# Unread 512-column bfloat16 products in TensorE's order, from the routing stage to the first slots

## The chip, the cores and the metric

The program runs on one core of a Trainium2 chip. The metric is the device time of one execution in microseconds. Three runs of the kernel before gave 3014.59, 3015.5 and 3016.41 us, a median of 3015.5 us.

## The reference, cut to what matters

Four layers are added to `x` (8 x 256 tokens of 256 numbers) one after the other. The first is attention with a context of 1601 rows, the second an expert layer with two of eight experts, the third a masked attention over the context, and the fourth an expert layer in which each token goes to one expert of eight. Only the fourth is touched:

```
x = _layernorm(x)
route = sigmoid(x @ router_w)                 # 2048 x 8
max_ind = argmax(route, axis=1)
max_prob = route[max_ind]
for e in range(8):
    h = silu(x @ gate_w[e]) * (x @ up_w[e])   # 256 -> 512
    out = out + where(max_ind == e, h @ down_w[e], 0)   # 512 -> 256
out = out * max_prob
```

## The kernel before, in words

The program is a row of blocks. In a block each engine has its own list of instructions, and between two blocks all engines meet at a barrier. Two blocks matter here.

`route_to_slots` decides which token goes to which expert. The 2048 tokens lie as 16 tiles of 128. VectorE (DVE) and GpSimd (POOL) make mean and deviation, and VectorE writes the normalised tiles `xn`. TensorE (PE) works in eight turns of two tiles. `turn(g)` (L2376 to L2383) transposes four 128x128 pieces into `ps_t`, ScalarE (ACT) copies them to `xt` (L2416), and four products with `router_w`, eight columns wide, put the router's sums into `ps_l` (L2392). A float32 product is two passes on the array, so that the trace has eight records for these four. `turn(g + 1)` stands ahead of the products of turn g, and so ScalarE's copy lies beside TensorE's work.

Then ScalarE applies the sigmoid (L2418), and VectorE picks each token's best expert and writes `onehot_bf`. TensorE counts the tokens of each expert (`ps_n`, L2397 and L2399, one and 16 products in bfloat16). VectorE turns the counts into a slot and a lane for each token: at most 23 slots of 128 rows, each of one expert. TensorE collects by 16 float32 products (`ps_f`, L2407) which token stands where, and VectorE writes `read_at` and `write_at` from it. Meanwhile SyncE (SP) has issued the loads of all expert weights, 12 MB (L2270).

`moe_slots` works through the 23 slots. GpSimd gathers the 128 rows of a slot by an indirect DMA (L2458), VectorE normalises them (`xn`, L2559), TensorE transposes them (`turn_x`, `ps_x`, L2480), ScalarE copies them, and TensorE multiplies by the gate and up weights (`hidden`, `ps_g` and `ps_u`, L2492), transposes the hidden rows (`ps_h`, L2501) and multiplies by the down weights (`ps_y`, L2509). The list of TensorE opens with `turn_x(0)`, `turn_x(1)`, a wait for the weights, and `hidden(0)`.

TensorE takes its instructions strictly in the written order. It stands at a wait until the semaphore has its value, and whatever stands ahead of an instruction must be through before it.

Of the kernel before, what the change touches and what calls it, by code (L numbers as in the profile page):

```python
# [14 lines left out]
P = 128  # L15
# [2191 lines left out]
def route_to_slots(nc, x_sb, router_dram, weights_dram, weights, w_loaded, mean_var, rstd, half, ident, upper_bf, ones_bf, iota,  # L2207
# [3 lines left out]
    with ExitStack() as ctx:  # L2211
        sb, psum, sem = scope(ctx, nc)
# [36 lines left out]
        ps_l = psum("ps_l6", [P, NT * E1])  # L2249
        ps_n = psum("ps_n6", [P, (NT + 1) * E1])  # L2250
        ps_f = psum("ps_f6", [P, FACTS * ESLOTS])

        router_loaded, upto_ready, tokens_made = sem("router6_loaded"), sem("upto6s"), sem("tokens6_made")
        xn_ready, xt_ready, xt_copied, logits, scored = sem("xn6s"), sem("xt6s"), sem("xt6_copied"), sem("logits6"), sem("scored6")
# [9 lines left out]
        with nc.Block() as block:  # L2264
            @block.sync
            def _(sp):
                sp.dma_start(router[:, :, :], router_dram.rearrange("(c p) e -> p c e", p=P)).then_inc(router_loaded, 16)

                for dst, src in zip(weights, weights_dram):
                    sp.dma_start(dst[:, :, :, :], src.rearrange("e (c p) n -> p e c n", p=P)).then_inc(w_loaded, 16)  # L2270
# [100 lines left out]

            @block.tensor
            def _(pe):
                pe.wait_ge(router_loaded, 16)

                def turn(g):  # L2376
                    pe.wait_ge(xn_ready, 2 * g + 2)
                    if g >= 2:
                        pe.wait_ge(xt_copied, g - 1)
                    for t in range(2):  # L2380
                        for c in range(DC):
                            last = nc.tensor.transpose(ps_t[:, g % 2, (t * DC + c) * P:(t * DC + c + 1) * P], xn[:, 2 * g + t, c * P:c * P + P], ident[:, :])
                    last.then_inc(xt_ready, 1)  # L2383

                turn(0)
                for g in range(NT // 2):
                    if g + 1 < NT // 2:
                        turn(g + 1)
                    pe.wait_ge(xt_copied, g + 1)
                    for t in range(2):  # L2390
                        for c in range(DC):
                            last = nc.tensor.matmul(ps_l[:, (2 * g + t) * E1:(2 * g + t + 1) * E1], xt[:, g % 2, (t * DC + c) * P:(t * DC + c + 1) * P],  # L2392
                                                    router[:, c, :], start=c == 0, stop=c == DC - 1)
                    last.then_inc(logits, 1)

                pe.wait_ge(is_own_bf, 1)
                nc.tensor.matmul(ps_n[:, 0:NT * E1], upper_bf[:, :], onehot_bf[:, :, :].rearrange("p t e -> p (t e)"), start=True, stop=False, skip_group_check=True)  # L2397
                for t in range(NT):
                    last = nc.tensor.matmul(ps_n[:, (t + 1) * E1:].rearrange("p (n e) -> p n e", e=E1), ones_bf[:, :],  # L2399
                                            onehot_bf[:, t:t + 1, :].to_broadcast([P, NT - t, E1]), start=False, stop=t == NT - 1, skip_group_check=True)  # L2400
                last.then_inc(counted, 1)

                pe.wait_ge(facts_ready, 1)
                for t in range(NT):
                    if t % NORM_TILES == 0:
                        pe.wait_ge(in_lanes, t // NORM_TILES + 1)
                    last = nc.tensor.matmul(ps_f[:, :], in_lane[:, t, :], facts[:, t, :, :].rearrange("p n s -> p (n s)"), start=t == 0, stop=t == NT - 1)  # L2407
                last.then_inc(held, 1)
# [15 lines left out]
                    norm_rstd(nc, pool, mean_var, rstd, half, norm, part)  # L2424


def moe_slots(nc, x_rows, rows_written, weights, out_rows, ident, read_at, write_at, fact, expert_of, w_loaded):

    gate_w, up_w, down_w = weights
    RING = 6  # L2430
# [1 line left out]
    with ExitStack() as ctx:  # L2432
        sb, psum, sem = scope(ctx, nc)
# [9 lines left out]
        ps_g = psum("ps_g7", [P, 512])  # L2443
        ps_u = psum("ps_u7", [P, 512])
        ps_h = psum("ps_h7", [P, 512])
        ps_y = psum("ps_y7", [P, 2, 512])

        gathered = [sem(f"gathered7_{j}") for j in range(RING)]
# [5 lines left out]
        with nc.Block() as block:  # L2454
# [18 lines left out]
            @block.tensor  # L2473
            def _(pe):
                def turn_x(s):
                    pe.wait_ge(xn_ready, s + 1)
                    if s >= 1:
                        pe.wait_ge(xt_copied, s)
                    for c in range(DC):
                        last = nc.tensor.transpose(ps_x[:, c * P:c * P + P], xn[:, s % 2, c * P:c * P + P], ident[:, :])  # L2480
                    last.then_inc(xt_ready, 1)

                def expert(s):
                    return pe.value_load(expert_of[0:1, s:s + 1], min_val=0, max_val=E1 - 1)

                def hidden(s, e):
                    pe.wait_ge(xt_copied, s + 1)
                    if s >= 1:
                        pe.wait_ge(hid_ready, s)
                    for ps, w, done in ((ps_g, gate_w, gate_done), (ps_u, up_w, up_done)):  # L2490
                        for c in range(DC):
                            last = nc.tensor.matmul(ps[:, :], xt[:, s % 2, c, :], w[:, bass.ds(e, 1), c, :].rearrange("p a n -> p (a n)"),  # L2492
                                                    start=c == 0, stop=c == DC - 1)
                        last.then_inc(done, 1)

                def turn_h(s):
                    pe.wait_ge(hid_ready, s + 1)
                    if s >= 1:
                        pe.wait_ge(ht_copied, s)
                    for c in range(HC1):  # L2500
                        last = nc.tensor.transpose(ps_h[:, c * P:c * P + P], hid[:, c * P:c * P + P], ident[:, :])  # L2501
                    last.then_inc(ht_ready, 1)

                def output(s, e):
                    pe.wait_ge(ht_copied, s + 1)
                    if s >= 2:
                        pe.wait_ge(made_ready, s - 1)
                    for c in range(HC1):
                        last = nc.tensor.matmul(ps_y[:, s % 2, 0:D], ht[:, c, :], down_w[:, bass.ds(e, 1), c, :].rearrange("p a n -> p (a n)"),  # L2509
                                                start=c == 0, stop=c == HC1 - 1)  # L2510
                    last.then_inc(y_done, 1)

                turn_x(0)
                turn_x(1)
                pe.wait_ge(w_loaded[0], w_loaded[1])
                hidden(0, expert(0))
                turn_h(0)
                hidden(1, expert(1))
                for s in range(ESLOTS):
                    e = expert(s)  # L2520
                    if s + 2 < ESLOTS:
                        e_ahead = expert(s + 2)
                        turn_x(s + 2)
                    output(s, e)
                    if s + 1 < ESLOTS:
                        turn_h(s + 1)
                    if s + 2 < ESLOTS:
                        hidden(s + 2, e_ahead)
# [62 lines left out]
def program(nc, x_dram, ctx_dram, ctx_t_dram, mask_dram, wq, wk, wv, wo, wk_ctx, wv_ctx, q_norm_w, k_norm_w,  # L2591
# [6 lines left out]
    x_rows = nc.dram_tensor("x_rows_scratch", (TOK, D), F32).ap()  # L2598
    with ExitStack() as ctx:
        sb, _, sem = scope(ctx, nc)  # L2600
        x_sb = sb("x_sb", [P, NT, D])
        ident = sb("ident", [P, P])
        ident_bf = sb("ident_bf", [P, P], BF16)
        iota = sb("iota", [P, P])
        upper_bf = sb("upper_bf", [P, P], BF16)
        ones_bf = sb("ones_bf", [P, P], BF16)
# [9 lines left out]
        with ExitStack() as context_ctx:  # L2616
# [5 lines left out]
            with ExitStack() as attention_ctx:  # L2622
# [8 lines left out]
        rows_written = sem("rows_written")  # L2631
# [5 lines left out]
        read_at = sb("read_at", [P, ESLOTS], U32)  # L2637
        write_at = sb("write_at", [P, ESLOTS], U32)
        fact = sb("fact", [P, FACTS, ESLOTS])
        expert_of = sb("expert_of", [P, ESLOTS], U32)  # L2640
        w_loaded = sem("w6_loaded")
        route_to_slots(nc, x_sb, router_w, (gate_w, up_w, down_w), (gate_sb, up_sb, down_sb), w_loaded, mean_var, rstd, half, ident, upper_bf, ones_bf, iota,
                       read_at, write_at, fact, expert_of)
        moe_slots(nc, x_rows, (rows_written, 16 * NT), (gate_sb, up_sb, down_sb), out_dram.rearrange("b l d -> (b l) d"),
                  ident, read_at, write_at, fact, expert_of, (w_loaded, 3 * 16))


# [35 lines left out]
```

## Time and profile before

| | us |
|---|---|
| median of three runs | 3015.5 (3014.59 to 3016.41) |
| the profiled execution, whole | 3013.14 |
| its span, first to last instruction | 3011.3 |
| TensorE busy | 2865.1 (95%) |
| VectorE busy | 2089.1 (69%) |
| ScalarE busy | 1993.3 (66%) |
| GpSimd busy | 1686.2 (56%) |

The mean granted clock of TensorE over the span is 0.977, where 1.00 is 2.4 GHz and 0.50 is 1.2 GHz. All times of the trace are microseconds from the start of the span. "PE" are matmuls, "PEld" the loading of the stationary operand. The end of a matmul is modelled, and matmuls are pipelined: the start of the next one tells its pace better than its own duration.

### The profile page before, as it was taken

The numbers are of one execution on the slowest core, as the hardware profiler recorded it, in microseconds if no ns is written. First come the engines' busy times: TensorE is split into PE (matmuls) and PEld (weight loads), VectorE is DVE, ScalarE is ACT, GpSimd is POOL, SyncE is SP. The second block draws the span as 40 slices with busy tenths as digits, with TensorE's granted clock in tenths as the row PEclk, the third lists the DMA queues.
The fourth block names the chain that finished last, engine by engine and source line by source line (L and its number), as shares of the span: only waits on it lengthen the run. The fifth ranks groups of instructions, "written<-read, shape, count | busy, mean of one in ns | idle before, by whom it ended". The sixth has DMA issues, their size and how long they took to land. (4 is left out here: it accounts for less than half of the span.)

```text
span 3011.3 us, 58598 instructions
## 1 busy us (share of the span) xinstructions
PE 2865.1 (95%) x18733; PEld 2451.1 (81%) x18733; DVE 2089.1 (69%) x4511; ACT 1993.3 (66%) x4950; POOL 1686.2 (56%) x2119
## 2 busy tenths in 40 slices
PE   7989999799999999999999999999999998699698
PEld 5768888688888888888888888888888875488655
DVE  7974455677777777777777777777777768656544
ACT  5656666677777777777777777777777639666211
POOL 6766663456556555655655565565556436465132
PEclk9999999999999999999999999999999989899699
DMA  5456767421111111111111111111111010354510
GB/s 182 136 159 205 209 205 220 137 68 55 41 68 42 54 41 69 54 41 68 43 53 41 68 54 41 68 44 52 41 68 54 1 48 1 106 153 125 179 42 26
DMA packets 249669, 253.40 MB, mean 84 GB/s; under 512 B 12470, under 2 KB 225599, under 8 KB 249376
## 3 DMA queue, kind: packets, MB, share of 16 engines
q1 hardware_dynamic: 229856, 228.92, 23.4%
q10 hardware_dynamic: 17312, 15.73, 1.8%
q0 software_dynamic: 2208, 5.12, 0.6%
q8 instruction: 150, 2.46, 0.3%
q14 instruction: 143, 1.17, 0.1%
HBM read 165.71 MB, written 84.93 MB: 83 GB/s over the span
## 5 line engine op out<-in xcount | busy, mean ns | idle before, releaser
L1027 ACT ACTIVATE w_hi<-ps_t 128x512 fp32r<-128x512 f32 (+2 forms) x1024 | 569.9, 557 | 415.3 <-PE ps_t L1267 412.0
L1097 DVE TENSOR_REDUCE piece_max<-ps_s 128x1 f32<-128x512 f32 (+2 forms) x1024 | 631.8, 623 | 257.4 <-PE ps_s L1254 229.7
L1123 DVE TENSOR_TENSOR w_lo<-ps_t,w_hi 128x512 fp32r<-128x512 f32 (+2 forms) x1024 | 656.4, 641 | 200.0 <-ACT w_hi L1027 183.7
L1287 PE MATMUL ps_o<-w_hi,v_hi 128*128 128x256 f32 (+1 forms) x1856 | 595.8, 321 | 0.0
L1194 POOL TENSOR_SCALAR prob<-prob,inv_sum 128x512 f32<-128x512 f32 (+2 forms) x768 | 477.3, 641 | 195.7 <-DVE inv_sum L1113 195.7
L1289 PE MATMUL ps_o<-w_hi,v_lo 128*128 128x256 f32 (+1 forms) x1856 | 523.5, 282 | 0.0
L1288 PE MATMUL ps_o<-w_lo,v_hi 128*128 128x256 f32 (+1 forms) x1856 | 522.3, 281 | 0.0
L1015 ACT ACTIVATE prob<-ps_s,neg_max 128x512 f32<-128x512 f32 (+2 forms) x768 | 487.3, 635 | 44.0 <-DVE neg_max L1104 35.2
L1267 PE MATMUL ps_t<-ident,prob 128*128 128x128 f32 (+1 forms) x2784 | 515.8, 272 | 0.0
L1249 PE MATMUL ps_s<-k_hi,q_hi 128*128 128x512 f32 (+2 forms) x1024 | 403.7, 394 | 27.6 <-ACT prob L1015 18.3
L1267 PEld LDWEIGHTS ps_t<-ident,prob 128*128 128x128 f32 (+1 forms) x2784 | 359.7, 140 | 52.4 <-issue 0.2
L1254 PE MATMUL ps_s<-k_hi,q_lo 128*128 128x512 f32 (+2 forms) x1024 | 396.8, 388 | 0.0
L1250 PE MATMUL ps_s<-k_lo,q_hi 128*128 128x512 f32 (+2 forms) x1024 | 376.8, 368 | 0.0
L1288 PEld LDWEIGHTS ps_o<-w_lo,v_hi 128*128 128x128 f32 (+1 forms) x1856 | 353.8, 191 | 0.0
L1287 PEld LDWEIGHTS ps_o<-w_hi,v_hi 128*128 128x128 f32 (+1 forms) x1856 | 351.9, 190 | 0.0
L1289 PEld LDWEIGHTS ps_o<-w_hi,v_lo 128*128 128x128 f32 (+1 forms) x1856 | 350.1, 189 | 0.0
L1209 POOL TENSOR_TENSOR v_lo<-raw_v,v_hi 128x512 fp32r<-128x512 f32 x124 | 149.1, 1212 | 203.8 <-ACT v_hi L1043 203.8
L1249 PEld LDWEIGHTS ps_s<-k_hi,q_hi 128*128 128x128 f32 x1024 | 194.2, 190 | 68.1 <-ACT prob L1015 47.0
L1202 POOL TENSOR_TENSOR k_lo<-raw_k,k_hi 128x480 fp32r<-128x480 f32 x124 | 148.5, 1217 | 159.4 <-ACT k_hi L1036 159.4
L1267 PE MATMUL ps_t<-ident,first_prob 128*128 128x128 f32 (+1 forms) x928 | 230.3, 272 | 1.4 <-DVE w_lo L1123 1.2
L1254 PEld LDWEIGHTS ps_s<-k_hi,q_lo 128*128 128x128 f32 x1024 | 196.9, 192 | 22.5
L1250 PEld LDWEIGHTS ps_s<-k_lo,q_hi 128*128 128x128 f32 x1024 | 195.1, 191 | 2.9
(291 smaller groups left out, 6208.4 us busy)
## 6 DMA issues: line engine op xcount, KB each, us to landing
v_scratch<-v_out SPq DMA_DIRECT2D x120, 256.0 KB, 3.0
raw_k<-k_scratch SPq DMA_DIRECT2D x32, 960.0 KB
raw_v<-v_scratch SPq DMA_DIRECT2D x32, 960.0 KB
k_scratch<-k_out SPq DMA_DIRECT2D x104, 256.0 KB, 2.7
q_scratch<-out_t SPq DMA_DIRECT2D x64, 256.0 KB, 2.5
r_all<-r_scratch SPq DMA_DIRECT2D x32, 512.0 KB
raw_q<-q_scratch SPq DMA_DIRECT2D x32, 512.0 KB
first_prob<-in_ctx_t ACTq DMA_DIRECT2D x50, 256.0 KB, 2.8
```

The lines of the kernel that those rows point to most:

```text
L1015: nc.scalar.activation(prob[n % PB][:, lo:hi], ps_s[:, p, lo - p * PC:hi - p * PC], ACT.Exp, bias=neg_max[:, n % PB:n % PB + 1], accum_out ...
L1027: nc.scalar.activation(pt_hi[keys, k % RING, cols], ps_t[keys, k % 2, cols], ACT.Copy).then_inc(hi_done, 1)
L1097: nc.vector.tensor_reduce(piece_max[:, n % 2, p:p + 1], ps_s[:, p, lo - p * PC:hi - p * PC], AX.X, ALU.max).then_inc(max_ready, 1)
L1123: nc.vector.tensor_tensor(pt_lo[keys, k % RING, cols], ps_t[keys, k % 2, cols], pt_hi[keys, k % RING, cols].bitcast(F32), ALU.subtract).th ...
L1194: nc.gpsimd.tensor_scalar(prob[n % PB][:, lo:hi], prob[n % PB][:, lo:hi], inv_sum[:, n % PB:n % PB + 1], 1.0, ALU.mult, ALU.mult).then_inc ...
L1249: nc.tensor.matmul(out, q_hi[gi][:, h, qs], k_hi[gi][:, lo:hi], start=True, stop=False)
L1250: nc.tensor.matmul(out, q_hi[gi][:, h, qs], k_lo[gi][:, lo:hi], start=False, stop=False)
L1254: nc.tensor.matmul(out, q_lo[gi][:, h, qs], k_hi[gi][:, lo:hi], start=False, stop=True).then_inc(scores_ready, 1)
L1267: last = nc.tensor.transpose(ps_t[0:keys, k % 2, at:at + P], prob[(2 * u + j) % PB][:, blk * P:blk * P + keys], ident[:, :])
L1287: nc.tensor.matmul(out, v_hi[gi][keys, vs], pt_hi[keys, k % RING, cols], start=blk == (0 if qt else 1), stop=False)
L1288: nc.tensor.matmul(out, v_hi[gi][keys, vs], pt_lo[keys, k % RING, cols], start=False, stop=False)
L1289: last = nc.tensor.matmul(out, v_lo[gi][keys, vs], pt_hi[keys, k % RING, cols], start=False, stop=blk == KB - 1)
```

## The change

In the routing block TensorE gets a helper that issues a given number of matmuls of `ones_bf` (128 columns, read four times, so 512 columns) with `upper_bf` as stationary operand. They go to a bank of its own, `ps_idle`, which nobody reads, and they wait for nothing and signal nothing. Ten stand at the head of the block, three behind the router products of each of the eight turns, 22 more behind the last turn, and 26 behind the counting. In the slots' block the same helper gives 24 ahead of `turn_x(0)` and two ahead of `turn_x(1)`. That is 108 products in all. Nothing is removed, no wait is added, and no other engine's instructions change.

```
@@ route_to_slots, block.tensor
+                def keep_clock(count):
+                    for _ in range(count):
+                        nc.tensor.matmul(ps_idle[:, :].rearrange("p (a n) -> p a n", a=4), upper_bf[:, :], ones_bf[:, :].unsqueeze(1).to_broadcast([P, 4, P]), start=True, stop=True)
+
+                keep_clock(10)
                 pe.wait_ge(router_loaded, 16)
...
                     last.then_inc(logits, 1)
-
+                    keep_clock(3)
+
+                keep_clock(22)
                 pe.wait_ge(is_own_bf, 1)
...
                 last.then_inc(counted, 1)
 
+                keep_clock(26)
                 pe.wait_ge(facts_ready, 1)
@@ moe_slots, block.tensor
+                keep_clock(24)
                 turn_x(0)
+                keep_clock(2)
                 turn_x(1)
```

The order on TensorE at the head of the routing block (`ps_t` are the transposes of the turns, `ps_l` the router's products). Before:

```order
L2372 UNCONDITIONAL_BRANCH
L2382 MATMUL ps_t<-ident,xn 128x128 x8
L2392 MATMUL ps_l<-router,xt 128x8 x4
L2382 MATMUL ps_t<-ident,xn 128x128 x4
L2392 MATMUL ps_l<-router,xt 128x8 x4
```

Now, on the same engine and at the same place:

```order
L2373 UNCONDITIONAL_BRANCH
L2378 MATMUL ps_idle<-ones_bf,upper_bf 128x512 x10
L2389 MATMUL ps_t<-ident,xn 128x128 x8
L2399 MATMUL ps_l<-router,xt 128x8 x4
L2378 MATMUL ps_idle<-ones_bf,upper_bf 128x512 x3
L2389 MATMUL ps_t<-ident,xn 128x128 x4
```

The ten stand ahead of the first turn's wait, and each later turn has three in front of it.

The order on TensorE between the last router products and the counting (`ps_n`). Before:

```order
L2382 MATMUL ps_t<-ident,xn 128x128 x4
L2392 MATMUL ps_l<-router,xt 128x8 x8
L2397 MATMUL ps_n<-onehot_bf,upper_bf 128x128
L2399 MATMUL ps_n<-onehot_bf,ones_bf 128x128
L2399 MATMUL ps_n<-onehot_bf,ones_bf 128x120
```

Now:

```order
L2399 MATMUL ps_l<-router,xt 128x8 x4
L2378 MATMUL ps_idle<-ones_bf,upper_bf 128x512 x3
L2399 MATMUL ps_l<-router,xt 128x8 x4
L2378 MATMUL ps_idle<-ones_bf,upper_bf 128x512 x25
L2406 MATMUL ps_n<-onehot_bf,upper_bf 128x128
```

The products of the last two turns are parted by three, and 25 (3 and 22) stand ahead of the counting.

The order on TensorE from the end of the counting over `ps_f` to the slots' first rows (`ps_x`). Before:

```order
L2399 MATMUL ps_n<-onehot_bf,ones_bf 128x8
L2407 MATMUL ps_f<-facts,in_lane 128x92 x16
L2264 UNCONDITIONAL_BRANCH
L2473 UNCONDITIONAL_BRANCH
L2480 MATMUL ps_x<-ident,xn 128x128 x4
L2484 TENSOR_LOAD expert_of
```

Now:

```order
L2408 MATMUL ps_n<-onehot_bf,ones_bf 128x8
L2378 MATMUL ps_idle<-ones_bf,upper_bf 128x512 x26
L2417 MATMUL ps_f<-facts,in_lane 128x92 x16
L2265 UNCONDITIONAL_BRANCH
L2484 UNCONDITIONAL_BRANCH
L2527 MATMUL ps_idle<-ones_bf,upper_bf 128x512 x24
L2491 MATMUL ps_x<-ident,xn 128x128 x2
L2527 MATMUL ps_idle<-ones_bf,upper_bf 128x512 x2
L2491 MATMUL ps_x<-ident,xn 128x128 x2
L2495 TENSOR_LOAD expert_of
```

Two of the additions stand in front of work that waits for VectorE, and nothing of them stands across the barrier (the two branches).

## Rows read from the trace of the kernel before

**Rows 1.** Windows of the last stages: span, busy (count) of PE, PEld, DVE, ACT, POOL, granted clock, DMA, GB/s

```profile
2809.40:2813.00 3.60, 0.00 (x0) 0.00 (x0) 2.09 (x9) 0.00 (x0) 0.15 (x1) 1.00 0.25 46
2815.50:2835.60 20.10, 20.06 (x96) 19.78 (x96) 7.89 (x33) 6.06 (x9) 3.39 (x5) 0.50 1.04 387
2835.60:2840.50 4.90, 0.02 (x1) 0.00 (x0) 4.18 (x52) 0.28 (x1) 0.00 (x0) 0.50 1.09 350
2841.80:2848.00 6.20, 0.00 (x0) 0.01 (x1) 5.72 (x18) 0.00 (x0) 0.00 (x0) 0.50 1.00 317
2848.00:2855.10 7.10, 7.08 (x32) 6.89 (x32) 2.64 (x7) 0.00 (x0) 0.00 (x0) 0.50 0.02 6
2876.00:2996.00 120.00, 120.00 (x456) 74.25 (x455) 56.74 (x102) 19.94 (x41) 36.99 (x38) 1.00 0.13 37
```

**Rows 2.** Timeline of the turns: start, duration, engine, line, [idle before it <- what ended it]

```profile
2815.54 1.94 PE L2382 MATMUL ps_t<-ident,xn 128*128 128x128 f32 x8 [6.21 <-DVE xn L2284]
2819.05 1.09 PE L2382 MATMUL ps_t<-ident,xn 128*128 128x128 f32 x4
2819.94 1.71 PE L2392 MATMUL ps_l<-router,xt 128*128 128x8 f32 x8
2821.50 1.09 PE L2382 MATMUL ps_t<-ident,xn 128*128 128x128 f32 x4
2822.02 1.38 DVE L2284 TENSOR_SCALAR xn<-x_sb,mean_var,rstd 128x256 f32<-128x256 f32 x4 [0.26 <-POOL rstd L104]
```

**Rows 3.** Timeline from the last turn to the end of routing

```profile
2832.45 0.60 ACT L2416 ACTIVATE xt<-ps_t 128x512 f32<-128x512 f32 x1 [1.86 <-PE ps_t L2382]
2833.06 1.28 ACT L2418 ACT_TABLE_LOAD   x1
2835.66 0.28 ACT L2418 ACTIVATE score<-ps_l 128x128 f32<-128x128 f32 x1 [1.32 <-PE ps_l L2392]
...
2840.53 0.29 PE L2397 MATMUL ps_n<-onehot_bf,upper_bf 128*128 128x128 bf16 x1 [4.91 <-DVE onehot_bf L2304]
...
2847.19 2.49 DVE L2348 TENSOR_TENSOR in_lane<-iota,lane 128x512 f32<-128x512 f32 x4
...
2848.02 7.10 PE L2407 MATMUL ps_f<-facts,in_lane 128*128 128x92 f32 x32 [6.27 <-DVE in_lane L2348]
```

**Rows 4.** Timeline of the slots' start

```profile
2861.76 0.69 PE L2480 MATMUL ps_x<-ident,xn 128*128 128x128 f32 x2 [6.64 <-DVE xn L2559]
...
2864.35 3.65 PE L2492 MATMUL ps_g<-gate_w,xt 128*128 x4 [0.27 <-issue]
...
2867.84 1.88 PE L2492 MATMUL ps_u<-up_w,xt 128*128 x4
...
2876.94 0.60 PE L2501 MATMUL ps_h<-ident,hid 128*128 128x128 f32 x4
...
2877.38 1.88 PE L2492 MATMUL ps_g<-gate_w,xt 128*128 x4
```

**Rows 5.** Timeline of PE in the second layer: 512-column bfloat16 products

```profile
2575.82 0.59 PE L1682 MATMUL ps_h<-xbt,w_bf 128*128 128x512 bf16 x2
2576.25 0.59 PE L1689 MATMUL ps_h<-xbt,w_bf 128*128 128x512 bf16 x2
```

**Rows 6.** Windows around clock changes in the second and third layers

```profile
2584.00:2587.80 3.80, 1.50 (x11) 0.65 (x9) 1.05 (x3) 3.74 (x8) 0.00 (x0) 1.00 0.01 2
2591.00:2594.60 3.60, 2.87 (x13) 1.12 (x12) 0.30 (x1) 1.94 (x4) 0.00 (x0) 0.50 0.00 0
2594.80:2598.00 3.20, 0.00 (x0) 0.00 (x0) 2.20 (x5) 0.00 (x0) 0.00 (x0) 1.00 0.00 0
2629.00:2632.00 3.00, 1.64 (x16) 1.40 (x14) 2.72 (x7) 2.14 (x6) 2.97 (x2) 1.00 1.07 367
2629.00:2636.00 7.00, 5.52 (x43) 4.78 (x42) 4.19 (x9) 5.28 (x11) 5.95 (x4) 1.00 1.07 352
```

**Rows 7.** DMA issues: KB, us from issue to landing; and the issue on SP's queue

```profile
down_w<-in_down_w SPq DMA_DIRECT2D x1, 4096.0 KB, 31.9
...
2817.16 10.69 SPq L2270 DMA_DIRECT2D down_w<-in_down_w  x1
```

More of the change, by code:

```diff
@@ L2251, in route_to_slots @@
         ps_f = psum("ps_f6", [P, FACTS * ESLOTS])
+        ps_idle = psum("ps_idle6", [P, 512])
         router_loaded, upto_ready, tokens_made = sem("router6_loaded"), sem("upto6s"), sem("tokens6_made")
@@ L2424, in _, with moe_slots @@
                     norm_rstd(nc, pool, mean_var, rstd, half, norm, part)
-def moe_slots(nc, x_rows, rows_written, weights, out_rows, ident, read_at, write_at, fact, expert_of, w_loaded):
+def moe_slots(nc, x_rows, rows_written, weights, out_rows, ident, read_at, write_at, fact, expert_of, w_loaded, upper_bf, ones_bf):
     gate_w, up_w, down_w = weights
@@ L2445, in moe_slots @@
         ps_h = psum("ps_h7", [P, 512])
+        ps_idle = psum("ps_idle7", [P, 512])
         ps_y = psum("ps_y7", [P, 2, 512])
@@ L2511, in output, with keep_clock @@
                     last.then_inc(y_done, 1)
+                def keep_clock(count):
+                    for _ in range(count):
+                        nc.tensor.matmul(ps_idle[:, :].rearrange("p (a n) -> p a n", a=4), upper_bf[:, :], ones_bf[:, :].unsqueeze(1).to_broadcast([P, 4, P]), start=True, stop=True)
+                keep_clock(24)
                 turn_x(0)
+                keep_clock(2)
                 turn_x(1)
@@ L2644, in program @@
         moe_slots(nc, x_rows, (rows_written, 16 * NT), (gate_sb, up_sb, down_sb), out_dram.rearrange("b l d -> (b l) d"),
-                  ident, read_at, write_at, fact, expert_of, (w_loaded, 3 * 16))
+                  ident, read_at, write_at, fact, expert_of, (w_loaded, 3 * 16), upper_bf, ones_bf)
 def kernel(x, ctx_2048, mask_BxS2_bk0, L0_xattn_wq, L0_xattn_wk, L0_xattn_wv, L0_xattn_wo, L0_xattn_wk_ctx, L0_xattn_wv_ctx,
```

## The prediction

> **What bounds the kernel now.** I read the page's slices first: TensorE is busy for 95% of the span, and the granted clock falls below full speed in few places. Then I cut the last stages into windows. In the slots TensorE is busy in all of 120 us at clock 1.00 [rows 1]: nothing ahead of them can hide behind them, so a microsecond saved before the first slot's hidden product is one off the end. The stage ahead is another picture. From 2815.5 to 2855.1 the granted clock is 0.50, which is 1.2 GHz [rows 1]. TensorE sets the pace in the eight turns (20.06 of 20.10 us busy) and in `ps_f` (7.08 of 7.10); in between it waits 4.91 us for VectorE's choice of the expert and 6.27 us for the lanes [rows 3]. Ahead of it TensorE had had nothing to do since 2809.4; in 2809.4 to 2813.0 the clock was still 1.00, and in the turns it was 0.50 [rows 1, 2]. The clock came back only in the first slot, between 2864.35 and 2867.84 [rows 4]. The question is thus whether the 108 products keep the clock at 2.4 GHz from 2811 on, and whether they delay what stands behind them.
>
> **Price of one added product.** Four bfloat16 products of 512 columns at full clock stand in two rows: the first two start at 2575.82, the next at 2576.25 [rows 5], 0.43 us for two, 0.215 us for one. At half the clock I take twice that, 0.43 us, as the gate products show, whose pace goes from (2867.84 - 2864.35)/4 = 0.87 us to 1.88/4, about 0.45 us [rows 4].
>
> **The ten at the head.** TensorE waits until 2815.54 for `xn` [rows 2]. The block begins at about 2811.4, which I estimate from 2809.4 and the VectorE work inside the first window [rows 1]; 10 x 0.215 = 2.15 us end at about 2813.6, 1.9 us before `xn` is there. Cost nothing, and at half the clock 4.3 us would end at 2815.7, a cost of 0.2 us.
>
> **The turns.** A turn is now 2821.50 - 2819.05 = 2.45 us: four transposes 0.89, eight records of products 1.56 [rows 2]. At full clock four transposes take 2877.38 - 2876.94 = 0.44 us [rows 4], half. No row shows the eight-column products at full clock. Bounds: they don't get faster (1.56, their own row) or they halve like the transposes (0.78). I take 0.78, since both pay the loading of a 128-column float32 operand at the array's pace. Three added ones are 0.65, so a turn is 0.44 + 0.78 + 0.65 = 1.87 us. The first two turns' transposes start at 2815.54 as before; they end at 2816.4, the copy (0.60, rows 3) lies behind the first of them, and the first products run 2816.9 to 2817.7, their three added ones to 2818.3. Six turns of 1.87 lead to 2829.5, and the last products end at 2830.3, with their tail at about 2830.6. Before it was 2835.6 [rows 1]. I book 4.8 us. VectorE doesn't stop this: its last four tiles are done at 2823.4 [rows 2], turn 4 starts at 2822.1 and needs tiles 8 and 9, which come out before those four, and turn 7 starts at 2827.7. ScalarE's copy and table load take 1.9 us behind the last transposes [rows 3]; from 2828.4 that is 2830.3, just in time. If the products don't halve, a turn is 2.65 us and this term is a loss of about 1 us.
>
> **The 25 behind the last turn.** They take 5.4 us, and the gap from the tail of the last product to `ps_n` is 4.91 us [rows 3]; they start some 0.25 us before that tail, so `ps_n` is late by about 0.3 us. The counting itself (2840.53 to 2841.80, rows 1 and 3) halves and gives back 0.6. Net gain 0.3 us. **The 26** take 5.6 us and the gap is 6.27 [rows 3]: no cost, but at half the clock they take 11.2 and cost 4.9.
>
> **`ps_f`.** 32 records take 7.1 us at clock 0.50 [rows 3]. At full clock 3.6, a gain of 3.5 us. VectorE feeds it in four pieces of 2.49/4 = 0.62 us, while eight records need 0.9 us, so it isn't starved. Bounds 0 (the clock is lost) and 3.6.
>
> **The slots' start.** The barrier and the gathers are as long as before. TensorE comes out of the barrier about 4.3 us ahead of the first `ps_x`, an estimate: of the 6.64 us idle ahead of it [rows 4] some 2.3 lie before the barrier opens. The 24 take 5.2 us, so `turn_x(0)` is late by 0.9 us. But `hidden(0)` isn't held by it: it waited for the second gather and `turn_x(1)`, and stood 2.6 us behind the first `ps_x` [rows 4]; that slack takes up the delay. Then the four `ps_g` records run at 0.43 in place of 0.87: gain 1.8 us. Bounds: -0.9 (the slack isn't there and the clock is low anyway) and 1.8.
>
> **The sum.** 4.8 + 0.3 + 3.5 + 1.8 = 10.4 us. The weights don't cut it: the last load was issued at 2817.16 and landed 31.9 us later, at 2849.1 [rows 7], while `hidden(0)` would come at 2864.35 - 8.6 = 2855.7. From the profiled execution's 3013.14 us that gives 3002.7. The median is 2.4 us above that execution; on the scale of the runs I say 3005 us.
>
> **Rivals.**
>
> *The clock falls in the first gap and comes back late (the one that ends on the other side).* The ten leave a hole of 1.9 us until `xn` and are followed by transposes and then another short wait for the copy; the first three dense ones come at 2817.7. The clock fell once after a stretch in which TensorE had 1.50 us of bfloat16 products in 3.80 us at 1.00 [rows 6], which is about as thin as 2811.4 to 2817.7 will be. Against it: in 2629 to 2632 TensorE had 1.64 us of work in 3.00, largely short float32 transposes, and kept 1.00 to 2636 [rows 6]. If it falls, a turn is 0.89 + 1.56 + 3 x 0.43 = 3.74 us; the last products end 8 us later than before, the 25 run at 0.43 for the first 3.5 us (as long as dense work ran before the rise in rows 4) and end 2.3 us later than the gap allows, and from there the gains of 0.5, 3.5 and 1.8 come. Net +4.5 us, 3019.6 us; it is a loss from the point at which more than about five of the eight turns run at the low clock. If the clock also falls across the barrier, 1.8 more, 3021.5.
>
> The Trainium skill ("TensorE: Matmul & The Clock Gate", Part 4: PE-mode transpose) speaks for this rival: it says that the full clock does not engage for transposes, which do not count as the engine being busy in the same way. By that rule the transposes would do nothing in the hole, and the time would be the 3019.6 just worked out. The trace doesn't settle it: the turns at 0.50 agree [rows 1], the kept clock from 2629 speaks against it [rows 6].
>
> *The clock falls, but the three per turn bring it back within a few turns, or it falls only across the barrier.* bfloat16 products that filled 2.87 of 3.60 us did bring it back [rows 6], but in a slow turn only 1.29 of 3.74 us are dense. Each two slow turns cost 3.7 us; one such pair leaves a gain of 6.7, 3008.8 us.
>
> *The products do not lift the clock at all.* They multiply constants. Then turns, 25, 26 and 24 all run at 0.43: 8 + 5.8 + 4.9 + 6 = about +24 us, 3039. The dense bfloat16 stretch in rows 6 after which the clock was 1.00 speaks against it.
>
> *The gain is eaten.* The small products don't get faster (the turns lose 1 us in place of gaining 4.8) and only `ps_f` and the slots' start gain: about 4.5 us, 3011 us.
>
> **How the numbers follow.** Forecast 0.60, with its own range 3002 to 3010; clock back early 0.12; clock late 0.17; gain eaten 0.07; no lift 0.04. A change within 0.2% (6 us) is about what a measurement of this kernel can't tell from none. Faster: 0.60 + 0.12 = 0.72. Same: 0.07 and 0.12 of the late clock, 0.19. Slower: 0.05 of it and 0.04, 0.09. The range runs from 3001 to 3020: below it 0.05, above it 0.13.
>
> **What would show it.** Right: a granted clock of 1.00 from 2809 to the end in the profile after, a turn of about 1.9 us, `ps_f` in 3.6 us, the first four `ps_g` at 0.43 each, `ps_n` some 5 us earlier and the first `ps_g` records some 8.6 us earlier, and idle TensorE time ahead of `ps_n` gone. Wrong: turns at 0.50 with 3.7 us each, the added products at 0.43 each, or a clock that falls around 2816 or across the barrier. If the turns run at 1.00 and are still longer than 2.4 us, the eight-column products are what I have wrong.

## The result, and the profile after

The changed kernel takes 3022.25 us (median of 7 runs, 3021.02 to 3027.27), the kernel before 3014.96 on the same chip: ratio 1.0027, 95% interval 1.0015 to 1.0038. It is slower, where I forecast 10 us faster. The profiled execution took 3026.97 us. The seven runs form two groups, three at 3026.97 to 3027.27 and four at 3021.02 to 3022.25; the profile is of the first group, and there is none of the second.

Of the two profiled executions, the routing block begins at 2811.37 before and at 2818.30 after. Those 6.9 us arise ahead of the block, in stages whose instructions are the same in both kernels, and the last section comes back to them. To compare the rest I use one measure: from the first GpSimd instruction of the routing block to the first gate product of the second slot ("the stretch"). Before it is 60.09 us, after 66.98. What follows it is 139.86 us in both. So the change costs 6.9 us in the stretch, in agreement with the medians (7.3).

TensorE's timeline after, in the order of the program (start, duration, what waited):

```profile
2818.33 2.32 PE L2378 MATMUL ps_idle<-ones_bf,upper_bf 128*128 128x512 bf16 x10 [2.05 <-PEq L57]
2822.48 1.21 PE L2389 MATMUL ps_t<-ident,xn 128*128 128x128 f32 x8 [1.84 <-DVE xn L2285]
2823.80 1.74 PE L2399 MATMUL ps_l<-router,xt 128*128 128x8 f32 x8
2825.39 1.44 PE L2378 MATMUL ps_idle<-ones_bf,upper_bf 128*128 128x512 bf16 x3
2826.62 1.06 PE L2389 MATMUL ps_t<-ident,xn 128*128 128x128 f32 x4
2827.47 1.71 PE L2399 MATMUL ps_l<-router,xt 128*128 128x8 f32 x8
2829.04 1.44 PE L2378 MATMUL ps_idle<-ones_bf,upper_bf 128*128 128x512 bf16 x3
2830.27 1.06 PE L2389 MATMUL ps_t<-ident,xn 128*128 128x128 f32 x4
...
2850.11 7.81 PE L2378 MATMUL ps_idle<-ones_bf,upper_bf 128*128 128x512 bf16 x25
2857.75 0.22 PE L2406 MATMUL ps_n<-onehot_bf,upper_bf 128*128 128x128 bf16 x1
...
2864.79 3.78 PE L2417 MATMUL ps_f<-facts,in_lane 128*128 128x92 f32 x32 [0.65 <-DVE in_lane L2349]
2870.88 7.03 PE L2527 MATMUL ps_idle<-ones_bf,upper_bf 128*128 128x512 bf16 x24 [2.31 <-PEq L57]
```

And windows of the same execution (columns as in [rows 1]):

```profile
2818.30:2820.60 2.30, 2.27 (x10) 0.90 (x10) 2.27 (x11) 0.00 (x0) 0.43 (x3) 1.00 0.36 27
2820.70:2822.40 1.70, 0.00 (x0) 0.00 (x0) 1.70 (x10) 0.00 (x0) 1.34 (x3) 1.00 1.01 351
2822.50:2823.90 1.40, 1.30 (x9) 0.89 (x9) 1.40 (x6) 0.75 (x2) 0.70 (x1) 1.00 0.97 364
2824.00:2850.10 26.10, 26.10 (x109) 20.97 (x109) 6.33 (x28) 5.19 (x8) 2.63 (x4) 0.50 1.06 377
2850.10:2854.60 4.50, 4.50 (x12) 1.62 (x13) 3.71 (x51) 0.28 (x1) 0.00 (x0) 0.50 1.01 322
2854.70:2857.70 3.00, 3.00 (x15) 1.37 (x14) 0.38 (x2) 0.00 (x0) 0.00 (x0) 1.00 0.06 20
2868.60:2870.80 2.20, 0.00 (x0) 0.00 (x0) 0.87 (x5) 0.00 (x0) 0.00 (x0) 1.00 0.00 0
2871.80:2875.10 3.30, 3.30 (x9) 1.09 (x8) 0.38 (x1) 0.00 (x0) 2.69 (x3) 0.50 0.21 57
```

The clock was still up under the ten and over the idle time behind them, and down from 2824 on, just behind the first transposes. A turn now takes 2830.27 - 2826.62 = 3.65 us, against 2.45 [rows 2]. In all of 26 us TensorE is busy and at half clock. The 25 bring the clock back about 4.5 us after they begin. It falls once more around the barrier: it is still 1.00 in the 2.3 us in which TensorE has nothing, falls some 0.8 us into the 24, and stays at 0.50 for about 3.4 us of them. They take 2877.74 - 2870.88 = 6.9 us in place of 5.2.

| part of the stretch | before | after | forecast |
|---|---|---|---|
| block begin to the end of the last router products | 24.0 | 31.8 (+7.8) | -4.8 |
| from there to `ps_n` | 5.1 | 7.6 (+2.5) | +0.3 |
| `ps_n` to `ps_f` | 7.5 | 7.0 (-0.5) | -0.6 |
| `ps_f` to the slots' block | 9.4 | 6.1 (-3.3) | -3.5 |
| slots' block to the second slot | 14.0 | 14.4 (+0.4) | -1.8 |

The kernel before has no TensorE instruction at the start of the slots' block. Its share of the last two rows is therefore taken from the run with the slots' products alone, where the block starts 9.42 us behind the first `ps_f`. The third and fourth rows came as forecast. The first and the last turned from gains into losses, and the small loss of the second grew.

### The profile page after: what moved, and what is told of

Same layout as the page of the kernel before. It is cut to its first block and busy times, and to the rows that moved or that the text cites. A ratio compares the mean times of both kernels' runs of the same rounds, so it can differ in the third digit from the quotient of the medians.

```text
span 3025.1 us, 58814 instructions
## 1 busy us (share of the span) xinstructions
PE 2896.8 (96%) x18841; PEld 2463.0 (81%) x18841; DVE 2089.4 (69%) x4511; ACT 1996.4 (66%) x4950; POOL 1691.8 (56%) x2119
```

## Experiments

Theory A was: the clock is lost in the hole behind the ten (the idle time until the first `xn`), and the rest follows from that. Rivals: B, the turns let it fall whatever stands ahead; C, the products cost time wherever they stand. All kernels ran beside runs of the kernel before on the same chip, and the ratio is to these. The stretch is that of the one profiled execution of each.

| kernel | median us (before) | ratio, 95% interval | stretch us |
|---|---|---|---|
| before | | | 60.1 |
| the change | 3022.25 (3014.96) | 1.0027, 1.0015 to 1.0038 | 67.0 |
| 19 at the head | 3007.0 (3015.9) | 0.9971, 0.9962 to 0.9981 | 50.3 |
| without the three per turn | 3012.51 (3015.9) | 0.9986, 0.9976 to 0.9995 | 56.8 |
| the three per turn alone | 3024.18 (3015.9) | 1.0027, 1.0015 to 1.0038 | 69.4 |
| 22 and 26 alone | 3014.05 (3015.9) | 0.9995, 0.9986 to 1.0005 | 59.7 |
| 19, none per turn | 3011.5 (3015.32) | 0.9987, 0.9978 to 0.9997 | 54.4 |
| 19, one per turn | 3011.45 (3015.32) | 0.9980, 0.9970 to 0.9990 | 51.9 |
| 10, six per turn | 3014.22 (one run) | none | 60.2 |
| 24 and 2 alone | 3016.63 (3015.32) | 1.0007, 0.9998 to 1.0017 | 61.3 |
| fitted groups | 3005.53 (3015.94) | 0.9963, 0.9949 to 0.9977 | 49.6 |
| 19 at the head again | 3005.71 (3015.94) | 0.9960, 0.9946 to 0.9974 | 50.3 |
| nine moved | 3009.74 (3015.94) | 0.9977, 0.9967 to 0.9988 | 53.6 |
| 17 transposes | 3006.92 (3015.8) | 0.9969, 0.9956 to 0.9982 | 50.3 |

**19 at the head.**

```
-                keep_clock(10)
+                keep_clock(19)
```

> The change, with 19 products at the head of the routing block in place of 10, so that they end (19 x 0.215 = 4.1 us) just before the first normalised tile. Theory A (the clock is lost in the hole between the ten and the first turn, and the loss is that of the slow turns): the granted clock stays 1.00 through the turns, a turn is 1.9 us in place of 3.65, and the time is 8 to 11 us under the kernel before, about 3005 us. Rival B (the hole is not what decides: transposes and eight-column products let the clock fall in the turns themselves, whatever stands ahead): the clock falls inside the turns and the time stays near 3022 us. Rival C (the added products cost their time wherever they stand): a little above 3022 us.

This is what A gave, and not what B or C gave: 8.9 us under the kernel before, by one number in the program. Its timeline and windows:

```profile
2814.67 4.26 PE L2378 MATMUL ps_idle<-ones_bf,upper_bf 128*128 128x512 bf16 x19 [2.05 <-PEq L57]
2818.83 1.21 PE L2389 MATMUL ps_t<-ident,xn 128*128 128x128 f32 x8
...
2821.70 0.60 PE L2389 MATMUL ps_t<-ident,xn 128*128 128x128 f32 x4
2822.14 0.96 PE L2399 MATMUL ps_l<-router,xt 128*128 128x8 f32 x8
2822.95 0.81 PE L2378 MATMUL ps_idle<-ones_bf,upper_bf 128*128 128x512 bf16 x3
2823.60 0.60 PE L2389 MATMUL ps_t<-ident,xn 128*128 128x128 f32 x4
```

```profile
2818.80:2833.80 15.00, 14.90 (x118) 12.31 (x118) 7.87 (x33) 6.05 (x9) 3.38 (x5) 1.00 1.03 387
2850.10:2852.30 2.20, 0.00 (x0) 0.00 (x0) 0.87 (x5) 0.00 (x0) 0.00 (x0) 1.00 0.39 127
2852.40:2857.50 5.10, 5.10 (x24) 2.38 (x25) 0.41 (x1) 0.00 (x0) 3.42 (x4) 1.00 0.18 55
```

A turn is 1.90 us, four transposes 0.44 and the eight-column products 0.81: the halving that no row before showed. The clock is 1.00 across the barrier here.

**The parts alone.** Without the three per turn (`keep_clock(3)` taken out), the three per turn alone, only 22 and 26, only 24 and 2:

> The change without the three products per turn; 10, 22, 26, 24 and 2 stay. Theory A: the clock falls as before and a turn is 2.45 us again, so the last router products come 9 us earlier than in the changed kernel; the 22 run at 0.43 us for 3.5 to 7 us and delay the counting by 2 to 3.5 us; the counting and the collecting products then gain 0.5 and 3.4 us. Time 1 to 3 us under the kernel before, about 3013 us. Rival C (cost goes with the number of products, 84 of 108 stay): about 3020 us.

> Of the 108 products only the three per turn (24). Theory A: the clock is 0.50 throughout the turns, seven groups of three stand on the path at 1.2 us each, the eighth lies in VectorE's choice: 8.4 us over the kernel before, about 3023.5 us. Rival B' (three per turn suffice to lift the clock after a few turns): the clock rises within the turns and the time is at or below 3015 us. Rival C: 24 of 108, 1.6 us over the kernel before, 3017 us.

> Only the 22 ahead of the counting and the 26 ahead of the collecting products. Theory A: the turns as before (2.45 us), the clock rises 3.5 to 7 us into the 22, the counting is late by 2 to 3.5 us, the counting itself gains 0.5 and the collecting products 3.4 us; the clock falls again across the barrier, the first gate products are at 0.87 us as before. Time 0 to 2 us under the kernel before, about 3014 us. Rival C: 48 of 108 products, 3 us over the kernel before, 3018 us.

> Only the 24 ahead of the first rows and the two ahead of the second. Theory A: they start at the low clock, which rises 3.5 to 7 us into them; the 24 then end 2.5 to 4.5 us late against the first rows, of which 0.9 us is slack; the first gate products then save 1.7 us. Time within 1 us of the kernel before, or up to 2 us over it. If the fallen clock costs nothing here, 1.7 us under it.

The medians lie where A put them: 3.4 us under the kernel before (A said 1 to 3), 8.3 over, 1.9 under and 1.3 over. The first three are not where C put them, and for the fourth C had no price. Those of 22 and 26 alone and of 24 and 2 alone can't be told from no change. In the first, turns of 2.45 us are back and the 22 take 7.5 us. The three alone cost 9.3 us in the stretch. Of these, 8.3 are there when the counting begins (seven groups at about 1.2 us; the eighth hides in the wait for VectorE), and 1.0 comes in the first slot, where the clock rises only amid the first `ps_u` products and not ahead of them, as it did before. 22 and 26 bring the slots' first rows 1.3 us earlier: `ps_f` takes 3.78 us for its 32 records, which gives more than the late counting takes. But in the first slot the clock again rises that late, which takes back 0.9, and 0.4 is left. 24 and 2 cost 1.2 us, their first 5.2 us being at half clock:

```profile
2859.30:2864.50 5.20, 5.20 (x13) 1.85 (x14) 0.42 (x1) 0.00 (x0) 3.51 (x4) 0.50 0.17 50
2864.60:2867.00 2.40, 2.40 (x12) 1.12 (x11) 0.59 (x1) 0.00 (x0) 1.79 (x3) 1.00 0.33 97
```

**How many per turn.** 19 with none, 19 with one, 10 with six:

> 19 products at the head and none behind the turns (22, 26, 24 and 2 stay). Theory A1 (the hole alone decides; once the clock is up, transposes and router products at full pace keep it): the clock stays 1.00, a turn is 1.25 us, bounded by VectorE's tiles, and the time is 1 to 3 us under the kernel with 19 and three. Theory A2 (transposes and eight-column products can't keep the clock, the three per turn are needed): the clock falls within the first turns, most turns are 2.45 us, the 22 start at the low clock, and the time is 2 to 4 us under the kernel before.

> 19 products at the head and one behind each turn. A1: clock 1.00, a turn of 1.46 us, 1 to 3 us under the kernel with 19 and three. A2: the clock falls in the turns; a slow turn is 2.88 us and the time 0 to 2 us over that of 19 and none.

> The change with six products per turn in place of three. The clock falls in the hole as before. Theory A3 (a slow turn with three is too thin to bring the clock back, more would): the clock comes back within two or three turns, and the rest run at 2.5 us (0.44 + 0.8 + 6 x 0.215); time about 3018 to 3020 us. If even six don't bring it back, a slow turn is 4.9 us and the time some 8 us over the changed kernel, about 3030 us.

With none the clock held for the first turns and then fell. This is A2, with 3.8 us under the kernel before where it gave 2 to 4. So rival B holds for turns without the three: 19 at the head don't keep the clock by themselves.

```profile
2818.30:2822.90 4.60, 4.10 (x35) 3.61 (x34) 4.60 (x19) 1.78 (x3) 2.01 (x3) 1.00 1.02 384
2823.00:2835.70 12.70, 12.70 (x63) 12.70 (x64) 3.12 (x15) 4.27 (x6) 1.31 (x2) 0.50 1.04 387
```

With one it held through the turns of the profiled execution, at 1.46 us each. But it had fallen in the 19 ahead of them, behind the 2.06 idle us in front of the block, and it fell again behind the last turn:

```profile
2816.40:2819.70 3.30, 3.30 (x10) 1.11 (x8) 3.30 (x18) 0.00 (x0) 1.93 (x4) 0.50 0.79 218
2821.20:2833.10 11.90, 11.65 (x104) 10.95 (x103) 6.22 (x28) 5.59 (x9) 2.63 (x4) 1.00 1.05 390
2833.40:2836.70 3.30, 3.30 (x9) 1.21 (x8) 2.66 (x38) 0.34 (x2) 0.00 (x0) 0.50 1.06 389
```

So 19 at the head can lose the clock too, and the first transposes then start 1.6 us later. The ten times of this kernel spread from 3002.93 to 3014.54; whether one per turn is enough stays open. With six, the clock fell in the hole as in the changed kernel and came back within three turns, which three per turn never managed:

```profile
2817.30:2827.40 10.10, 10.10 (x38) 6.80 (x37) 7.06 (x31) 1.68 (x3) 2.62 (x4) 0.50 1.05 391
2827.50:2840.70 13.20, 13.20 (x97) 9.90 (x96) 0.00 (x0) 4.27 (x6) 0.00 (x0) 1.00 1.06 375
```

So twice as many products cost 6.8 us less in the stretch than three, in one run; I had expected 2 to 4.

**Is it the hole?**

```
                     if g + 1 < NT // 2:
                         turn(g + 1)
+                    if g == 0:
+                        keep_clock(9)
```

> As many products as with 19 at the head, but only 10 of them there; nine stand behind the transposes of the first two turns, ahead of the first router products. The hole between the ten and the first turn stays. Theory A (the hole decides): the clock falls at the end of the hole as in the changed kernel, the nine run at 0.43 us or a little faster, and the time is at least that of the changed kernel's distance, 6 to 9 us over the kernel before, unless the nine bring the clock back at once. Rival (it is the amount of work before and in the first turns that decides, wherever it stands): the clock stays 1.00 and the time is 6 to 8 us under the kernel before.

The edit leaves the ten at the head and puts nine more behind the transposes of the first two turns. Here my theory fell in the form in which I had stated it, and the rival of this run gave the time: 6.2 us under the kernel before. The 1.8 us hole is there and the clock is 1.00 over it and in all the turns:

```profile
2819.30:2821.10 1.80, 0.00 (x0) 0.02 (x1) 1.80 (x10) 0.00 (x0) 1.43 (x3) 1.00 0.87 332
2821.10:2824.10 3.00, 2.99 (x17) 1.86 (x18) 3.00 (x14) 1.18 (x2) 1.46 (x3) 1.00 1.04 397
2824.10:2837.70 13.60, 13.60 (x110) 11.44 (x109) 4.87 (x21) 4.87 (x7) 1.91 (x3) 1.00 1.04 387
```

So it is not the idle time by itself that decides. What fits both runs is the whole thin run from the end of the ten to the next wide (512-column) products: 2820.6 to 2825.4 in the changed kernel, idle time, transposes, a short wait and eight-column products in a row. Wide work at either end of it was enough. This version is 3.3 us longer in the stretch than with 19 at the head: the nine push the first router products back, which costs 1.6 us, and in the profiled execution the clock fell around the barrier, which costs 1.8.

**Do transposes count?**

```
                 keep_clock(10)
+                for _ in range(17):
+                    nc.tensor.transpose(ps_idle[:, 0:P], ident[:, :], ident[:, :])
```

> The change with the hole behind the ten filled with 17 float32 transposes of the identity (17 x 0.11 = 1.9 us), which nobody reads. If transposes count for nothing, as the page has it, the clock falls where it fell in the changed kernel and the time is 6 to 8 us over the kernel before. If they count as the bfloat16 products do, the clock stays 1.00 and the time is near that of 19 at the head, 8 to 10 us under the kernel before. In between (the clock stays in some executions): a median between the two with a wide spread.

They do, for keeping it. The clock stayed, and the six times lay between 3005.41 and 3009.31:

```profile
2818.60:2820.30 1.70, 1.70 (x17) 1.62 (x16) 1.70 (x10) 0.00 (x0) 1.34 (x3) 1.00 0.95 241
2820.40:2835.60 15.20, 15.09 (x120) 12.31 (x117) 8.17 (x34) 6.04 (x9) 3.67 (x5) 1.00 1.03 384
```

The sentence of the Trainium skill that I had set against the change (TensorE: Matmul & The Clock Gate, Part 4: PE-mode transpose) says that the full clock does not engage for transposes, as they do not count as the engine being busy in the same way. For keeping the clock this does not hold here: 17 float32 transposes back to back kept the granted clock at 1.00. Whether transposes also raise a clock that is down, no run shows. By that rule the time would have been 3019.6, on the right side of the kernel before, but for a reason that this run refutes.

The run also says what thin means. From the ten to the next wide products it has a stretch nearly as long as the changed kernel's, 4.2 us (2818.7 to 2823.0) against 4.8, and the clock held. So transposes back to back don't belong to the thin run; idle time and eight-column products do, and the turns without the three show that the latter, mixed with transposes, lose the clock with little idle time (4.10 of 4.60 us busy ahead of the fall).

**Fitted groups** (19, 3, 19, 28, four behind `ps_f`, 20, 2) beside 19 at the head once more:

> Groups fitted to the gaps read from the traces: 19 at the head, three per turn, 19 ahead of the counting (22 with the last turn's three), 28 ahead of the collecting products, four new ones behind these so that TensorE has work while VectorE finishes, 20 and 2 ahead of the slots' rows. Theory A: clock 1.00 to the end in most executions; the counting 0.5 us earlier than with 19/22/26/24, the first rows 0.8 us earlier, of which the second gather gives back most; the idle stretch across the barrier 2.3 us shrinks to about 1.5. Time 0.5 to 2 us under the kernel with 19 at the head and the rest unchanged. Rival: no difference that can be measured, since the second gather and not TensorE opens the slots.

> The change with 19 at the head once more, to be compared on one chip with the fitted groups and with the nine moved. 8 to 10 us under the kernel before.

The stretch is 0.7 us shorter, and the medians can't be told apart, as the rival says. The slots' first rows come 1.2 us earlier, but the second rows then wait 0.51 us for what the second gather brings, and the first gate products come only 0.8 us earlier. Both beat the kernel before by 0.4%.

## Why the prediction was wrong

**The step that failed** is the ten at the head: that ten products, ending 1.9 us before `xn`, keep the clock until the turns. The term of the sum that rested on it, 4.8 us gained in the turns, came out as 7.8 us lost. The ten cost nothing, as forecast (2.32 us, with 1.84 us of idle time behind), but they were there for the clock, and that was not kept: it is 0.50 from 2824.0 on. The main case weighed the hole of 1.9 us; the first wide products behind it come 4.8 us after the ten. Nine products more in that stretch, at either end, kept the clock. I had the comparison [rows 6] in front of me with both answers, took the one that kept the clock, and gave the other 0.17. The 4.8 itself is 0.2 short: 2835.6 less 2830.6 is 5.0.

**The turns.** The price of a turn at full clock was right: 1.87 forecast, 1.90 in the run with 19. At half clock, 3.74 in the rival and 3.65 measured, with the last products 7.8 us late, where I had 8. Three per turn are also too few to bring the clock back.

**The 25** were 2.5 us late, as in the rival (2.3). **The 26 and `ps_f`** were right: the clock was back by then, the 26 hid, and the gain was 3.3 of 3.5 us.

**The slots' start** was mis-sized: +0.4 in place of -1.8, because the clock fell across the barrier. With the clock kept it is -1.5 (12.56 us in the run with 19, against 14.0). The rival with this second fall is what happened. Its price was 3021.5, and the measured time is 0.75 us above it. Its own terms give a little more: 4.5 us over the median of 3015.5 are 3020.0, and 1.8 more are 3021.8.

**The range** ended at 3020, since I had given the rival too little and put its second price outside. So the mechanism that cost the time stood in the prediction, as a rival; what was wrong was to hold it for the less likely one.

With the clock kept the forecast of the whole holds: 10.4 us, against 9.8 in the stretch and 8.9 to 10.2 in the medians of the two runs with 19.

## What to carry to other kernels

Work that is put in to keep a clock has to be judged by the longest thin run that it leaves, idle time and very short products taken together, up to the next wide products or transposes back to back, and not by the idle time of one wait. How long such a run may be was not measured here. If the work fails to keep the clock it runs at half pace on the path: decide with the granted clock of a window after every group, and first give more work to the place where the gap is free. In this kernel nine products at the head were the difference between +7 us and -9 to -10 us.

## What the runs showed that I had not expected

- Float32 transposes kept the clock as well as 512-column bfloat16 products did in the same place (a stretch of 50.3 us in both).
- The stages before the change differ from execution to execution by as much as the change is worth. The routing block began at 2811.4, 2818.3, 2814.7 and 2812.4 us in the profiles of the kernel before, the change, 19 at the head and six per turn. The extra time arises where the clock is down for longer. Followed along VectorE's list of instructions, the change is behind the kernel before by 2.2 us at 40 us, by 3.4 at 240 us, by 6.7 at 580 us, and by 6.9 at the block. Around 219 us the clock was up before and still down after, and around 560 us it was down for some 13.4 us before and 23.5 after, in the same stages of the program.

Before:

```profile
219.00:222.00 3.00, 3.00 (x15) 2.48 (x14) 0.34 (x1) 1.19 (x2) 1.21 (x2) 1.00 1.09 354
553.60:567.00 13.40, 6.29 (x19) 4.35 (x17) 5.96 (x14) 2.82 (x5) 1.46 (x2) 0.50 0.50 157
```

After:

```profile
219.00:222.00 3.00, 3.00 (x8) 2.33 (x8) 0.69 (x1) 0.60 (x1) 0.17 (x1) 0.50 1.00 327
557.50:581.00 23.50, 13.73 (x38) 10.18 (x39) 9.40 (x23) 7.47 (x21) 3.55 (x6) 0.50 0.47 164
```

- Around a barrier of 2.3 idle us the clock fell in the change, with 19 and one per turn, and with the nine moved. It did not fall with 19 at the head, with 19 and none, without the three, with six per turn or with the 17 transposes, though `ps_f` and the 24 stood on the two sides in all of them. What decides this between executions stays open.
